# GpSimd issues the finished expert's scatters ahead of the next gathers

## The reference

```python
# h: the 2048 normalised tokens, 128 features each
logits = h @ router_weight.T
probs = softmax(logits)
topk_probs, selected = top_k(probs, 2)         # two experts a token
# for each expert: its up to 640 kept tokens, in slots
expert_inputs[e, slot] = h[token]
pre  = expert_inputs @ ff_pre_act_weight.T     # 128 -> 512
gate = expert_inputs @ gate_weight.T           # 128 -> 512
expert_out = (pre * silu(gate)) @ ff_post_act_weight.T   # 512 -> 128
out[token] += expert_out[e, slot] * kept_weight[token, e]
x = x + out
```

## Time and profile before

| what | value |
|---|---|
| median of 3 runs | 384.75 us (383.73 to 385.06) |
| span of the profiled execution, first to last instruction | 410.6 us |
| busiest engines over that span | PE 74%, DVE 71%, POOL 52%, ACT 35% |
| GpSimd's 40 scatter issues (L1197) | 62.9 us, 1572 ns each |
| GpSimd's 40 gather issues (L1180) | 38.7 us, 968 ns each |
| scatters, first to last start | 271.4 to 403.7 us |
| gathers, first to last start | 237.2 to 371.6 us |

### The profile page before, as it was taken

How to read it: one execution, slowest core, us unless ns; L and a number is a source line. 1 busy time by engine, 2 the same in 40 slices (tenths; PEclk the granted TensorE clock), 3 DMA queues, 4 the chain that set the end, 5 groups by cost and what they waited for, 6 DMA issues and landing times.

```text
span 410.6 us, 5169 instructions
## 1 busy us (share of the span) xinstructions
PE 305.2 (74%) x1465; PEld 212.9 (52%) x1465; DVE 290.1 (71%) x615; ACT 144.4 (35%) x285; POOL 211.5 (52%) x145
## 2 busy tenths in 40 slices
PE   5969996776798669766591866969695959597940
PEld 4635342333344335333261555959594949497940
DVE  5954999999999999999978843646363636362500
ACT  2535963223533353344042003333332323233320
POOL 0632455974455435543714062174848484848664
PEclk9965996887888878988786798978797979798995
DMA  6040024254000000000002011144443333323332
GB/s 186 2 102 0 0 52 102 62 140 164 14 13 0 26 26 0 0 26 26 0 27 77 1 41 26 32 92 76 72 85 59 79 62 86 55 48 43 29 26 25
DMA packets 20756, 20.31 MB, mean 49 GB/s; under 512 B 2624, under 2 KB 14848, under 8 KB 20736
## 3 DMA queue, kind: packets, MB, share of 16 engines
q1 hardware_dynamic: 13184, 14.63, 12.4%
q0 software_dynamic: 7040, 5.25, 10.3%
q10 hardware_dynamic: 512, 0.19, 0.3%
HBM read 10.82 MB, written 5.05 MB: 39 GB/s over the span
## 4 chain that ended last, share of the span: by engine, by line
PE 38%; DVE 25%; issue 13%; another core or an unknown queue 9%; POOL 7%; ACT 4%; DMA 1%; DVEq 1%; POOLq 1%; ACTq 0%
PE psum L1481 10%; DVE ring L518 8%; PE psum L1460 5%; PE psum L1315 5%; DVE ring L509 5%; PE psum L1462 5%; PE psum L1461 4%; POOL ring L1130 4%; PE psum L1298 2%; DVE sm L543 2%; POOL out L1197 2%; DVE xn L457 1%; POOL parts L1119 1%; PE psum L1295 1%
## 5 line engine op out<-in xcount | busy, mean ns | idle before, releaser
L1130 POOL TENSOR_TENSOR ring<-ring,cbc 128x1024 f32<-128x1024 f32 x31 | 74.9, 2416 | 85.7 <-DVE ring L518 85.7
L518 DVE TENSOR_TENSOR_SCAN ring<-ring 128x1024 f32<-128x1024 f32 x32 | 102.6, 3210 | 0.0
L1315 PE MATMUL psum<-ring,cst 128*128 128x512 f32 x128 | 76.4, 729 | 15.4 <-POOL ring L1130 15.3
L1298 PE MATMUL psum<-stack,sel_r 128*128 (+1 forms) x120 | 55.8, 572 | 25.4 <-DVE ring L509 24.7
L1197 POOL DMA_INDIRECT out<-ring,sid x40 | 62.9, 1572 | 16.9 <-issue 11.0
L1180 POOL DMA_INDIRECT ring<-rows,gid x40 | 38.7, 968 | 63.4 <-DVE gid L780 39.5
L817 DVE TENSOR_TENSOR ring<-psum,ring 128x320 f32<-128x320 f32 x64 | 31.4, 491 | 56.0 <-ACT ring L1048 30.6
L1460 PE MATMUL psum<-stack 128*128 128x320 f32 x128 | 47.6, 372 | 27.2 <-issue 16.4
L935 ACT ACTIVATE ring<-psum,nega 128x510 f32<-128x510 f32 x64 | 41.7, 681 | 46.1 <-PE psum L1298 44.4
L1048 ACT ACTIVATE ring<-psum 128x320 f32<-128x320 f32 x64 | 27.9, 438 | 78.7 <-PE psum L1462 50.8
L1298 PEld LDWEIGHTS psum<-stack,sel_r 128*128 128x128 f32 x120 | 25.1, 224 | 53.4 <-DVE ring L509 33.6
(11 more groups left out here) (180 smaller groups left out, 342.4 us busy)
## 6 DMA issues: line engine op xcount, KB each, us to landing
stack<-parts SPq DMA_DIRECT2D x16, 256.0 KB, 3.8
win_s<-in_wg SPq DMA_DIRECT2D x8, 256.0 KB
win_s<-in_w SPq DMA_DIRECT2D x8, 256.0 KB
w_s<-in_w SPq DMA_DIRECT2D x8, 256.0 KB
xt<-in_x SPq DMA_DIRECT2D x4, 256.0 KB, 4.7
out<-xt SPq DMA_DIRECT2D x4, 256.0 KB, 2.3
rows<-xn SPq DMA_DIRECT2D x4, 256.0 KB, 2.3
ring<-rows,gid POOLq DMA_INDIRECT x40
```

What stands on the lines that cost most here:

```text
L518: v.tensor_tensor_scan(hh[:, s].rearrange("p a b -> p (a b)"), da[:, s].rearrange("p a b -> p (a b)"), uu[:, s].rearrange("p a b -> p (a b ...
L1130: g.tensor_tensor(hc[:, s], hh[:, s], cb, ALU.mult).then_inc(s_product, 1)
L1298: ins = mm(bank(to + k), sel, stack[:, half, kind, bass.ts(c, CH)], start=True, stop=True)
L1315: ins = mm(bank(YB), wred[:, o:o + D], hc[:, s, k, :], start=(grp == 0), stop=(grp == NG - 1))
```

## The change

In GpSimd's `expert`, the five gathers for expert e + 2 are issued behind the five scatters of expert e, and no longer ahead of them. Nothing else differs; sixteen empty lines at the head of the file are gone, so that line n of the kernel before is line n - 16 of the changed one.

```diff
             def expert(e, b, more=True):
 
-                if more:
-                    gather_ready(e + 2, b)
-                    for q in range(NQ):
-                        gather(b, q)
                 pool.wait_ge(s_scatter_ids, 2 * e + 2)
                 for q in range(NQ):
                     pool.wait_ge(s_weighed, NQ * e + q + 1)
...
                     g.indirect_dma_start(out=out, out_offset=bass.IndirectOffsetOnAxis(ap=sid[:, b, q:q + 1], axis=0),
                                          in_=ye[:, b, q, :], in_offset=None, compute_op=ALU.add
                                          ).then_inc(s_scattered, 16)
+                if more:
+                    gather_ready(e + 2, b)
+                    for q in range(NQ):
+                        gather(b, q)
```

## The result

The changed kernel takes 444.26 us in the median of four runs (441.86 to 445.92), the kernel before 384.9 on the same chip (383.73 to 385.62): a ratio of 1.153, with a 95% interval of 1.148 to 1.159. The forecast was 433, with a range of 405 to 447. The profiled execution of after took 444.54 us, of which 442.5 are span, so its time is the span plus 2.0.

What follows compares the result with a forecast made beforehand. GpSimd's issuing was taken to bound a plain phase at 15.7 us, 94.2 for six; the change makes a 23.9 us chain, 0.7 + 9.4 + 5.1 + 2.7 + 4.4 + 1.6. So 384.75 + 143.4 - 94.2 gives 433 us, range 405 to 447.

Steps and rivals of the forecast that it cites:

- A: The forecast itself: plain phases of 15.7 us, bound by GpSimd, become 23.9; 423 to 449 us, chance 0.72.
- (a): Start of a phase, ScalarE's first gate to GpSimd's first scatter, through the first weighing: 0.7 us.
- (b): GpSimd's five scatter issues, now ahead of the gathers: 9.4 us a phase.
- (c): GpSimd's five gathers, up to the start of the last: 5.1 us a phase.
- (d): The last gather from its issue to its transpose on TensorE: 2.7 us, from two prologue cases of 2.5 and 3.6.
- (e): TensorE's last transpose to the next expert's first gate, at full clock: 4.4 us a phase.
- (f): TensorE's dense work slowed by half clock after its wait: 1.6 us a phase, the middle of 0 and 3.2.
- The base: Six plain phases before the change: 94.2 us, 15.7 each by GpSimd's issuing, late completions taken as the profiled execution's alone.
- The tail: End of the run: experts 6 and 7 have no gathers around their scatters, so it stays as it was: 0.
- B: Rival: TensorE's late completions are wholly or partly in plain runs too; 410.7 us, or 400 at best; chance 0.18.
- C: Rival: gathers stay hidden, as up keeps its slow pace for a cause other than gathers; 401 us or less; chance 0.05.
- D: Rival: faster, with late completions real and GpSimd's issues shorter in plain runs; 379 us for an 18.6 phase; chance 0.03.

Runs made afterwards that it cites:

- experiment 5: Changed kernel plus thrown-away TensorE matmuls on zeros before and between the transposes, except in expert 1's turn: 432.62 us, ratio 1.117 to the kernel before.
- Experiment 2: Changed kernel with two scatters ahead of the five gathers and three behind: 409.45 us, ratio 1.056 to the kernel before.
- experiment 7: experiment 6's kernel with VectorE's scatter list, and the wait for its buffer, moved behind up's eight products: 414.31 us, ratio 1.077 to the kernel before.
- experiment 1: The kernel before, unedited, profiled a second time: 387.18 us, beside a median of 386.71 us in its set.
- experiment 8: The kernel before with VectorE's scatter list written behind up's eight products: 384.42 us, ratio 0.998 to the kernel before.
- experiment 6: Changed kernel in which GpSimd waits for all five weighed tiles, then gathers, then scatters: 443.61 us, ratio 1.149 to the kernel before.
- experiment 3: Changed kernel with one scatter ahead of the five gathers and four behind: 404.54 us, ratio 1.045 to the kernel before.

## Why the prediction was right, and where it was off

The forecast, A, holds: plain phases that GpSimd bounds became a chain through it. It fell 11 us short, because the chain is 12.4 us longer than its sum, and it would have fallen further short but for a tail that I had put at nothing. Step by step, measured as means over the six phases of after:

| step | forecast | measured | in phase 6 |
|---|---|---|---|
| (a) first gate to first scatter | 0.7 | 1.60 | 389.28 to 390.90 |
| (b) five scatters | 9.4 | 9.41 | 390.90 to 400.28 |
| (c) five gathers to the last's issue | 5.1 | 5.10 | 400.28 to 405.37 |
| (d) landing | 2.7 | 3.37 | 405.37 to 408.90 |
| (e) last transpose to next gate, full clock | 4.4 | 4.39 | from experiment 5, mean of its six |
| (f) half clock | 1.6 | 2.10 | 408.90 to 415.18 (mean of the six 6.49) less (e) |
| a phase | 23.9 | 25.97 | 389.28 to 415.18 |

**The chain** was right in each of its links, and the two that were counted in issues, (b) and (c), to about 0.01 us. Experiment 2 shows the scatters on the path, 1.86 for each one ahead.

**(a) was mis-sized.** I let the scatter start as the weighing ended. GpSimd starts 0.93 later, in phase 6 from 389.97 to 390.90. In experiment 7 the same pause is 324.12 - 323.09 = 1.03, behind the fifth weighing. The trace of before had it too, on the gather of 304.78 in the earlier trace rows: the list that it waits for is ready at 303.82 (VectorE's timeline), 0.96 earlier, and I had not used the row.

```profile
303.65 0.17 DVE L780 TENSOR_SCALAR gid<-token 128x5 int32<-128x5 f32 x1
```

**(d) was mis-sized.** I took the shorter of the two landings of the earlier trace rows as the undisturbed one. The six of after are 2.83 to 3.56, five of them 3.40 or more, so the 3.6 of the earlier trace rows was the usual one, and the end of my range. Here the Trainium skill ("DMA: Bandwidth & Descriptors", section "Anatomy of one DMA — SWDGE (gpsimd) path"), by which I had estimated 2.15 for the 64 KB, does not agree with the trace: from the issue's start to the transpose's start, which is what the chain needs, not one of the six is that short, and even the first gather of phase 6, with no other gather in flight, takes 402.82 - 400.28 = 2.54.

**(f) was mis-sized.** I took half of the dense work at half clock. In four of the six phases the slow stretch is 13.7 us and covers all of it but the next up's first unit (413.91 in the windows above), in the two others it is 10.3 us and covers about half. The mean price, 2.10, lies between the middle, 1.6, and the end, 3.2. That end does not follow from my own rate: 4.0 us that take 1.6 times as long grow by 2.5. But the 1.6 was too small, since the clock rose at 299.70 within the sixteen matmuls that I read it from the earlier trace rows; 5.10 against 2.84 is 1.8 times, and with that 3.2 comes out.

These three, 0.9 + 0.7 + 0.5 = 2.1 a phase, are 12.4 us. **The base** was right as a sum: 94.2 for the six plain phases of before against 93.8 in experiment 1. What it rested on, that the late completions belong to one execution, was an argument; experiment 1 now shows a second profile of the same kernel without them. Two steps of the argument did not hold. A single phase can be shorter than 15.7 (12.5 in experiment 1), since scatters of one phase are still being issued in the next; only the six together are held. And that 24.3 came near the missing 25.9 was partly luck. Against experiment 1 the first profile is 25.3 us longer: 23.6 in the six phases, 6.0 ahead of them, where I had counted 1, and 4.4 less in the tail. I had also written that no other stretch has such waits; ScalarE's first two gates of all have one:

```profile
251.68 0.77 ACT L1048 ACTIVATE ring<-psum 128x320 f32<-128x320 f32 x2 [0.49 <-remote]
```

The Trainium skill's rule ("SBUF — State Buffer", section "SBUF: two separate sides"), that DMAs and engines do not share ports, agrees with experiment 1: gathers run beside up in it, and no gate is late.

**Who waits for scatters.** I had written that nobody waits for them within a phase. In the kernel before VectorE does, 17.8 us in all (experiment 1). It costs nothing there, by experiment 8, and in the changed kernel no such wait is left; but it decides experiment 6 and disturbs experiment 3.

**The tail** was not 0. From the first gate of expert 7 to the end of the span it is 31.9 us in experiment 1 and 27.3 after, 4.6 less. In the kernel before GpSimd comes to the last expert with scatters of the one before still to issue, and begins expert 6's at 359.08, 5.7 us behind the gate at 353.41; after, it begins 1.5 behind it. I had read the tail in the disturbed execution, where GpSimd had no such backlog. The balance, from experiment 1: 387.18 + (155.8 - 93.8) - 4.6 = 444.6, the time of the profiled execution of after (444.54). That is a balance of two single executions; from the median of before, 384.9, the same sum gives 442.3, and the last 2 us up to 444.26 are not accounted for. Runs of the kernel before spread from 382 to 389.

Of the rivals, B falls by experiment 1. C falls by TensorE's rows: gates follow each other at 0.89 and the gathers are waited for all the same. D falls since a scatter takes 1.55 to 1.62 in the profile and three of them 5.58 by experiment 2, from plain times alike (444.26 - 409.45 = 34.8, six times 5.8). What the signs named beforehand said came true in the main: gathers behind the fifth scatter with 0.3 idle, gates 0.9 apart, no "remote" wait, the clock at 0.5, though from 400.24 on and so ahead of the transposes. The first gates stand 25.3 to 26.9 apart, two of the six beyond the 22 to 26, and TensorE's wait up to the last transpose is 11.7 us where I had some 9.

## What to carry to other kernels

Before moving issues on an in-order queue, ask which of them feed another engine in the same turn and which only empty a buffer. In this kernel the feeding ones, put behind others, pay every issue ahead of them, 1.86 us a scatter, plus the wait of the first one, plus a landing that was covered before. Look also at who waits for the emptying ones one turn later (experiment 6: a buffer of five numbers per row cost 4 us a phase), for the order that is good for the one ring can be bad for the other. And when a profile's span and the plain time differ by several per cent, take a second profile of the same kernel before pricing anything that only the first one shows.

## What was not expected of the hardware

The one profiled execution ahead of the prediction showed TensorE's completions late at ScalarE, twelve times in six phases and by 1.5 to 4.9 us; none of the eleven other profiles of this study has a wait of that name. What did it stays open: no run brought it back, so none could take it away.

Where GpSimd stands waiting, it starts an indirect DMA some 0.9 to 1.0 us after the instruction that it waits for has ended, whether that is ScalarE's weighing (0.93, and 1.03 in experiment 7) or, in the kernel before, VectorE's list (0.96).

The granted clock did not come back as the dense work began again: in the changed kernel it stood at 0.50 for 13.7 us in four phases and 10.3 in two, in experiment 5, where TensorE had thrown-away matmuls in its wait, for some 3.3 us a phase, inside the wait, and at 1.00 in the dense work.
